# VectorE takes a slot's turned unit and residual ahead of the running maximum of the tile before

## The reference

```
# block 0
scale = cond @ norm_w.T + 1
h = x * scale * rsqrt(mean(x*x) + 1e-6)
val, gate = split(h @ up_w.T)                 # 2 x 2048 columns
h = val * gelu(gate)
hq = round(h * s) / s,  s = 127 / clip(max|h| over a row's 2048 values, 1e-5)
x = x + hq @ weight_quant(down_w).T           # weights -1, 0, 1 times their mean size
# block 1, for each batch b
Wd_b = Wd + 0.1 * (cond[b] @ Wdd.T + bdd),  Wu_b = Wu + 0.1 * (cond[b] @ Wdu.T + bdu)
x = x + relu(x @ Wd_b.T + bd) @ Wu_b.T + bu
```

## Time and profile before

| | |
|---|---|
| median of 3 runs | 940.36 us (938.34 to 940.86) |
| profiled execution, its own time | 937.38 us |
| its span | 935.2 us |
| TensorE busy | 921.9 us, 99% |
| VectorE busy | 687.5 us, 74% |
| GpSimd busy | 646.0 us, 69% |
| ScalarE busy | 427.2 us, 46% |
| chunks 1 to 6, some 107 us each | 110 to 752 us of the span |

### The profile page before, as it was taken

How to read it: one execution, slowest core, us unless ns; L and a number is a source line. 1 busy time by engine, 2 the same in 40 slices (tenths; PEclk the granted TensorE clock), 3 DMA queues, 4 the chain that set the end, 5 groups by cost and what they waited for, 6 DMA issues and landing times.

```text
span 935.2 us, 13874 instructions
## 1 busy us (share of the span) xinstructions
PE 921.9 (99%) x5002; PEld 452.1 (48%) x5002; DVE 687.5 (74%) x1034; ACT 427.2 (46%) x788; POOL 646.0 (69%) x565
## 2 busy tenths in 40 slices
PE   9999999999999999999999999999999999999997
PEld 6555544444444444444444444444444444455586
DVE  6778778867878678776878688686878665356676
ACT  7897667214742157123742257222751156215343
POOL 1000049899979998799988999799987999200664
PEclk9999999999999999999999999999999999999999
DMA  9999644655446553574346552584446526020584
GB/s 310 224 229 209 178 138 144 160 156 158 121 133 158 159 152 97 159 196 135 122 121 199 157 161 88 152 212 113 143 116 183 142 68 180 12 74 29 198 296 179
DMA packets 142059, 144.04 MB, mean 154 GB/s; under 512 B 51876, under 2 KB 89256, under 8 KB 141480
## 3 DMA queue, kind: packets, MB, share of 16 engines
q1 hardware_dynamic: 141992, 143.17, 53.7%
HBM read 112.46 MB, written 19.92 MB: 142 GB/s over the span
## 4 chain that ended last, share of the span: by engine, by line
PE 70%; POOL 8%; DVE 7%; issue 5%; DMA 5%; ACT 3%; SPq 2%; DVEq 0%; POOLq 0%; ACTq 0%
PE bank L1176 17%; PE bank L1178 17%; PE bank L1177 17%; POOL delta_reg L564 4%; PE bank L1280 4%; PE bank L1235 4%; DVE delta_reg L895 3%; POOL delta_reg L567 2%; DMA xr<-in_x 2%; DMA delta_reg<-in_L_cond_Wdd 2%; PE bank L1290 1%; POOL delta_reg L571 1%; PE bank L1417 1%; PE bank L1426 1%; PE bank L1447 1%
## 5 line engine op out<-in xcount | busy, mean ns | idle before, releaser
L564 POOL TENSOR_TENSOR delta_reg<-delta_reg,s_bc 128x512 f32<-128x512 f32 x256 | 334.3, 1327 | 91.7 <-DMA delta_reg<-in_L_cond_Wdu 78.7
L1176 PE MATMUL bank<-x_split,w_hi 128*128 128x512 f16 x1016 | 385.3, 379 | 0.9 <-DVE absrun L905 0.9
L1178 PE MATMUL bank<-x_split,w_lo 128*128 128x512 f16 x1016 | 385.1, 379 | 0.0
L1177 PE MATMUL bank<-x_split,w_hi 128*128 128x512 f16 x1016 | 385.1, 379 | 0.0
L710 ACT ACTIVATE bank<-h 128x512 f32<-128x512 f32 x126 | 75.7, 601 | 309.0 <-DVE h L1013 308.9
L895 DVE STREAM_TRANSPOSE delta_reg<-delta_reg 128x512 f32<-128x512 f32 x192 | 197.1, 1107 | 24.6 <-DMA delta_reg<-in_L_cond_Wdd 18.7
L567 POOL TENSOR_TENSOR delta_reg<-delta_reg 128x512 f32<-128x512 f32 x128 | 166.7, 1302 | 10.0
L1013 DVE SCALAR_TENSOR_TENSOR h<-bank,desc,g 128x512 f32<-128x512 f32 x128 | 94.7, 740 | 99.9 <-issue 54.7
L1176 PEld LDWEIGHTS bank<-x_split,w_hi 128*128 128x128 f16 x1016 | 99.4, 98 | 123.0 <-issue 8.2
L1178 PEld LDWEIGHTS bank<-x_split,w_lo 128*128 128x128 f16 x1016 | 99.4, 98 | 119.9
L1177 PEld LDWEIGHTS bank<-x_split,w_hi 128*128 128x128 f16 x1016 | 99.4, 98 | 112.1
(11 more groups left out here) (182 smaller groups left out, 754.6 us busy)
## 6 DMA issues: line engine op xcount, KB each, us to landing
delta_reg<-in_L_cond_Wdd SPq DMA_DIRECT2D x128, 256.0 KB, 2.9
delta_reg<-in_L_cond_Wdu SPq DMA_DIRECT2D x128, 256.0 KB, 3.2
qreg<-in_L_cond_up_w SPq DMA_DIRECT2D x32, 256.0 KB, 4.7
xr<-in_x SPq DMA_DIRECT2D x30, 256.0 KB, 4.2
x_scratch<-xr SPq DMA_DIRECT2D x30, 256.0 KB, 4.1
xn<-in_x SPq DMA_DIRECT2D x7, 1024.0 KB, 6.1
h<-in_L_cond_down_w SPq DMA_DIRECT2D x4, 1024.0 KB, 7.8
delta_reg<-in_L_cond_down_w SPq DMA_DIRECT2D x8, 512.0 KB, 4.6
```

Of the source, the lines that this page charges most:

```text
L564: pool.tensor_tensor(part_mul[:, b, :, :], part_w[:, i % 2, :, :], cond_all[:, 2 * pair + b, :].unsqueeze(1).to_broadcast([P, 4, C]), ALU. ...
L1176: pe.matmul(bank[:, :], w_hi[:, k, cols], xh[:, par, k, :], start=(k == 0), stop=False)
L1177: pe.matmul(bank[:, :], w_hi[:, k, cols], xl[:, par, k, :], start=False, stop=False)
L1178: mm = pe.matmul(bank[:, :], w_lo[:, k, cols], xh[:, par, k, :], start=False, stop=(k == KD - 1))
```

## The change

Two pieces of VectorE's program change places: in every slot but slot 0, the residual and the turned units now stand ahead of the running maximum of the tile before. The functions themselves are as they were.

```diff
                     if not first and j < 8:
                         quantise(c - 1, 2 * j)
-                    if j > 0:
-                        absolute_max(c, j - 1)
                     if not first and 10 <= j < 10 + TT:
                         residual(c - 1, j - 10, Y)
                     if j > 0 and not first:
                         turn_units(c, j)
+                    if j > 0:
+                        absolute_max(c, j - 1)
                     for i in parts_in(sum_slots, n):
                         sum_part(i)
```

## The result

| | before | after |
|---|---|---|
| median (lowest to highest), 10 runs each | 938.26 us (935.98 to 940.86) | 945.48 us (942.17 to 949.25) |
| ratio, 95% interval | | 1.0076 (1.0058 to 1.0094) |
| profiled execution, its span | 937.38, 935.2 us | 946.14, 943.9 us |

What follows compares the result with a forecast made beforehand. The prediction took TensorE's own work to bound the kernel. Costs of 4.07 us less gains of 3.51 us gave +0.56 us: 937.9 for the profiled execution, 940.9 on the timed runs' scale, range 938.3 to 943.8.

Steps and rivals of the forecast that it cites:

- What bounds the kernel.: Chunks 1 to 6: TensorE's own work sets the time; VectorE counts only where TensorE has nothing it may issue.
- The maximum comes later, 4.07 us.: Chunk 1 and slot 2 of chunks 3 to 6: value matmuls wait for the later maximum, costing 4.07 us.
- the price of the long wait: Chunk 1: value matmuls already waiting for the maximum wait 1.89 us more, as two turns now go first.
- turns and residuals come earlier, 3.51 us: Slots 2, 3, 10 and 14: TensorE's waits for turns and residuals shrink by at most 0.60 each, 3.51 us together.
- The part of slots 2 and 3: Products of slots 2 and 3, chunks 2 to 6: waits for the turns come back, 1.75 us together.
- The gain of 1.03 at the products of slot 14: Chunks 3, 4 and 6: earlier turns of slot 11 bring x and these products earlier, 0.16, 0.27 and 0.60 us.
- Nothing changes for GpSimd.: GpSimd's sums depend on L909, which stays behind both moved pieces in the same place, so no change for GpSimd.
- growth of chunk 1: Sign of being wrong: chunk 1 does not become about 1.9 us longer.
- holds by the maximum in slots 9 to 13: Sign of being wrong: the maximum holds TensorE there; the tightest slot, 9 of chunk 6, was given a margin of 1.5.
- Waits of the maximum for ScalarE are worth nothing.: VectorE's 32 such waits, 21.4 us, mostly go but gain nothing, since VectorE afterwards waits for TensorE's value matmuls.
- The rival that VectorE paces the stretch: Much faster: the 21.4 us of waits for ScalarE leave the path, giving 919; chance 0.01.
- The slower rival: Slots 1 and 2 of chunks 1 and 3 to 6: only the 4.07 us of costs come, giving 944.4; chance 0.13.

Runs made afterwards that it cites:

- the experiment: New order in slots 9 to 15 only, slots 1 to 8 as in the kernel before: 940.94 us, ratio 1.0017 to the kernel before.
- fillers in the wait: New kernel plus 40 small useless matmuls ahead of the long wait in slot 3 of chunk 1: 945.04 us, ratio 1.0058 to the kernel before.
- narrow and new: New kernel with GpSimd's products and sums over 8 of 128 numbers: 935.56 us, ratio 0.9951 to the kernel before.
- the narrow work: Kernel before with GpSimd's products and sums over 8 of 128 numbers, leaving out part of block 1's weights: 932.13 us, ratio 0.9914.
- old kernel with earlier loads: Kernel before with the two loads of a long slot's first unit issued ahead of the transposing DMAs in SyncE's queue: 946.83 us, ratio 1.0082.

## Why the prediction was wrong, by its own steps

- *What bounds the kernel.* Right. TensorE's even spacing left only its waits to price, and the loss is found in them.
- *The maximum comes later, 4.07 us.* Right in place and mechanism: the same five places. It was 4.83, since VectorE came to slot 2 up to 0.4 us later relative to TensorE than before (chunk 3: its L878 in slot 1 starts 1.40 behind the gates, before 1.01). No maximum holds TensorE in slots 9 to 13, as stated.
- *The step that failed first: the price of the long wait, which left out the clock.* I priced the wait of chunk 1 as a wait only. With 2.71 us idle in a row the granted clock fell to 0.50 for 3.4 us and cost 1.7 us more in the trace; that slot alone costs 3.5 by the medians, where I had 1.89. Before, the 0.93 did not do that. I had the length of the new wait (0.93 + 1.89) in my own sum and did not ask what TensorE does behind it.
- *The step that failed next: turns and residuals come earlier, 3.51 us.* The part of slots 2 and 3 was right (1.75, measured 1.65). The rest failed (a gain of 1.76 forecast, a loss of 1.6, 0.4 to 2.7, by the experiment): I let the fourth turn follow the first by a fixed time, but its load waits in SyncE's queue behind a transposing DMA. I also wrote that "0.60 less ahead of it and 0.60 more behind it leave L909 where it was"; the first 0.60 was not there, so L909 and the product behind it were late: in chunk 3 the L1013 of slot 9 starts 0.86 later than TensorE's own delay of 4.40 explains (392.42 against 387.16). The gain of 1.03 at the products of slot 14 hung on the load of x going out 0.6 earlier. Against the first gate matmul of slot 10 the one for slot 13 went out 0.61, 0.69, 0.42 and 0.88 later in chunks 3 to 6. How much of that the maximum of slot 9 makes is open: with the old order in these slots (slots 1 to 8 only) it was 0.39, 0.52, 0.74 and -0.04.
- *Nothing changes for GpSimd.* Wrong: its waits for the sums grew from 39.0 to 48.4 us. With the growth of chunk 1 by 3.1 us in place of 1.9 this is one of two signs of being wrong that the prediction named and that came; the third, holds by the maximum in slots 9 to 13, did not.
- *Waits of the maximum for ScalarE are worth nothing.* Right in price: they fell from 21.4 to 13.4 us (not to a few), and the kernel got slower. The rival that VectorE paces the stretch, to which the Trainium skill's rule on occupancy points ("Perfetto Trace Analysis", section Identifying the Most-Contended Engine), fell with it. The section names the share of useful multiplications (MFU) beside the share of weight loads; the prediction took the latter alone.
- *The rivals.* The slower rival named the right side, at 0.13. That its 944.4 lies near 945.48 is luck: it starts from the median of three runs, it gives nothing back where 1.65 came back in slots 2 and 3, and it has no clock in it. Its condition, a load not landed in slots 1 and 2, was not what happened there; in slot 9 a load did set the fourth turn. I had put the point of decision in slot 9 at a load "1.5 later than now", where a load that merely doesn't come earlier was enough.

By the medians the sum was 4.0 us too low in slots 1 to 8 (4.07 - 1.75 = 2.32 forecast, 6.3 measured) and 3.4 too low in slots 9 to 15. Of the 4.0 the trace of the new kernel explains 2.6: the clock 1.7, the maxima 0.8, the recoveries 0.1. The rest lies within the interval of that run and is not explained.

## What to carry to other kernels

When a step is moved ahead, follow each wait that it should shorten to what ends it: a transfer that an in-order queue issues behind something else does not come earlier, and the step that left the shadow of that wait then delays what stands behind it. When a change makes TensorE wait for some microseconds in one piece, price the matmuls behind the wait as well. A swap in a few chosen slots gained 2.5 us where the swap in all lost 7.1: it can gain where the waiting consumer (the products) asks first and lose where it asks for the other piece first, so choose it per slot.

## What the runs showed of the hardware

- TensorE, 2.71 us without a matmul, was granted 1.2 GHz for the next 3.4 us (granted clock 0.50); with 0.36 us (fillers in the wait), 0.93 (before) and 1.3 (narrow and new) it stayed at full speed. The mean clock of the new kernel was 0.997 to 0.999 in nine of ten runs, and 1.000 in one, which was the fastest (942.17). The Trainium skill says that idleness throttles the array ("TensorE: Matmul & The Clock Gate", section What's actually happening); the trace agrees.
- VectorE's subtraction of two SBUF tiles (L860) took 1455 ns beside GpSimd's full work and 760 ns beside the narrow work, and a step over 4 columns (L866) 493 against 193 ns. With GpSimd's work narrow the whole kernel was 8.1 us faster. The Trainium skill states that a VectorE step with two inputs in SBUF and a GpSimd instruction that reads SBUF take turns at a pair of ports, which the one that starts first holds for its whole instruction ("SBUF — State Buffer", section SBUF: two separate sides). The times of L860, which has two such inputs, agree with it; L866 has one, and no run here shows by which port GpSimd's work stretches it.
- Once, in chunk 2 of the old kernel with earlier loads, the issue of the load of x took 2.76 us in SyncE's queue, a little behind two transposing DMAs; the eleven others of these loads in chunks 1 to 6 of that kernel took 0.42 or 0.43. What made it long is not shown.
